# A LoRA feed-forward, grouped-query attention and top-4 mixture of experts in one kernel: the expert rows' table filled in the first stage, three accumulators with deeper rings, activations turned one block later, routing one tile earlier

## The chip, the cores and the metric

The kernel runs on one core of a Trainium2 chip as one program. The metric is the time on the device in microseconds (us); "before" is the median of three runs. The profile is of one execution of its own.

## The reference, cut to what matters

```python
# x: (32, 32, 256): 32 sequences of 32 tokens, T = 1024 tokens of D = 256
def cond(x, Wg, Wu, Wd, A*, B*, idx):        # LoRA with one of 8 adapters per sequence, rank 16, hidden 1024
    gate, up = lora(x, Wg, Ag, Bg, idx), lora(x, Wu, Au, Bu, idx)
    return lora(silu(gate) * up, Wd, Ad, Bd, idx)
def ffn(x, ...):
    h = rms(x, ln_w)
    q, k, v = h @ wq, h @ wk, h @ wv         # 32 heads, 8 kv heads of 64; rope on q and k
    o = softmax(causal(q @ k.T / 8)) @ v
    x = x + o @ wo
    h = rms(x, ff_ln_w)
    logits = h @ wg                          # 16 experts
    topv, topi = top_k(logits, 4)
    weights = scatter(softmax(topv), topi)
    a = silu(h @ w1[e]) * (h @ w3[e])        # for each expert e, 256 -> 256
    return x + sum_e weights[e] * (a @ w2[e])
out = x + ffn(cond(x))
```

## The kernel before, in words

Each engine has an instruction stream written by hand, and semaphores tie them. The order within an engine is the order of the code. Products in float32 are made of a high and a low part (`*_hi`, `*_lo`): three matmuls for one (`product`, L1322).

**Stage A**, to about 122 us: the LoRA feed-forward, on the tokens in two groups of 512. SP loads raw weights into `staging` (`raw`), POOL loads the same weights rounded (`load_hi`) and subtracts (`split`). The last loads of this stage are issued at 69 us; later only four more pieces (`wo_w` 2 and 3, `gate_w`) come through `staging`.

**Stage B**, to about 385 us: eight tiles of 128 tokens (four sequences each). `attend(t)` stands in every engine's stream. On TensorE it makes the scores of tile t, projects q, k and v of tile t + 1, turns the probabilities (`turn_p`), multiplies them with v (`heads_out`), turns the output (`turn_o`, into `oT_hi` by ScalarE and `oT_lo` by VectorE) and makes the output projection (`attention_out`) of tile t - 1. v goes through a DMA that spreads it over blocks by sequence (`spread_v` on SP's queue, into `v_blk`). Softmax works on `z`, which VectorE, POOL (a shift by the maximum) and ScalarE (exponential) touch in turn. For the mixture, older tiles are routed meanwhile: `logits(t - 3)` with `read_logits`, then for t - 4 `hits`, `ranks`, `place` (the position of each token within its expert's rows) and `gates_exp`, `gate_sum`, `pick` (the gate values), then for t - 5 `slots`, `gate_scale`, and on POOL `gates` and four `scatter`, indirect DMAs that write a tile's rows (256 values, 16 gates, the token's number in the row) into `moe_rows` in DRAM. This table has room for 1024 rows for each of 16 experts, and one block for strays, 16512 rows of 276 words. It must hold strays' numbers wherever no token is written, so it is filled beforehand: `fill_rows` on ScalarE's queue, two pieces of 16 x 128 rows in each of `attend(0)` to `attend(3)`, a ninth small one and `set_acc` in `attend(3)`.

**Stage C**, to about 425 us: `send`, `pick` and the others for the last tiles, written out after `attend(6)`; tile 7's attention is written out too.

**Stage D**: 47 blocks of 128 rows. The first 16 are one for each expert in fixed order, the other 31 take their expert and first row from a table that VectorE computes (`blk_exp`, `blk_rows`; `TABLE`, after the gate products of blocks 1 to 3). SP loads a block's rows (`xs<-moe_rows`, a ring of XSR = 6 buffers), TensorE turns them (`rows_in_turned`, L1680), ScalarE and VectorE split them, TensorE multiplies by w1 and w3 (`gate_up_e`, L1326, into `ringT`), ScalarE and VectorE make `mact`, TensorE turns it (`act_turn`, L1699) and multiplies by w2 (`down_e`, L1707). ScalarE scales by the gate (`scaled`, `y`, a ring of YR = 3), and POOL adds it to the accumulator of the block's number mod 2 with an indirect DMA (`moe_acc<-y,xs`, L633; `y_out`). A buffer of xs is free when that DMA has landed, since it holds the token numbers. `value_load` reads an expert's number into TensorE's registers (L1719). The order on TensorE:

```python
for b in range(NBLK + 2):
    if b + 1 < NBLK: rows_in_turned(b + 1)
    if 2 <= b: down_e(b - 2, expert_of(b - 2))
    if 1 <= b <= NBLK: act_turn(b - 1)
    if b < NBLK: gate_up_e(b, expert_of(b))   # expert_of(b): value_load where b >= 16
```

**The end**: SP loads accumulator 1 whole and accumulator 0 in quarters, VectorE adds the one to `resid` and that to the other, SP stores.

Of the kernel before, what the change touches and what calls it, by code (L numbers as in the profile page):

```python
# [14 lines left out]
ALU = mybir.AluOpType  # L15
# [22 lines left out]
MH = HID // P  # L38
NAD = 8
# [25 lines left out]
HXR, XSR, YR = 4, 6, 3  # L65
# [9 lines left out]
def build(nc, x, seq_adapter, cond_head, cond_w, qkv_w, wo_w, gate_w, expert_w, norms, consts, ff_row, route_tab, out):  # L75
    with ExitStack() as ctx:
# [23 lines left out]
        cst = sb("cst", [P, CCOLS])  # L100
        staging = sb("staging", [P, 2, MCOLS])
# [30 lines left out]
        act_hi, act_lo = pair("actp", [P, 2, GROUP])  # L132

# [8 lines left out]
        fill = sb("fill", [P, ROW])  # L142
# [48 lines left out]
        acc_rows = [nc.alloc_sbuf_tensor_at(f"acc_rows{i}", [P, NT, D], F32, offset=qkv_at + 4 * i * NT * D) for i in range(2)]  # L191
        cursor[0] = qkv_at + 4 * NE * WCOLS
        y = sb("y", [P, YR, D])
        mactT = sb("mactT", [P, KD * P])
        assert cursor[0] == probs_end
        ew2 = sb("ew2", [P, NE, W2COLS])
        xs = sb("xs", [P, XSR, ROW])
        xsT_hi, xsT_lo = pair("xsT", [P, 2, KD * P])
        msilu = sb("msilu", [P, D])
        mact = sb("mact", [P, D])  # L200
# [18 lines left out]
        acc_dram = [nc.dram_tensor(f"moe_acc{i}", (T + P, D), F32, kind="Internal").ap() for i in range(2)]  # L219
# [17 lines left out]
        hi_in = [sem(f"hi_in{i}") for i in range(NCH)]  # L237
# [34 lines left out]
        FILLS, ACC_SETS = 9, 3  # L272
# [17 lines left out]
        y_out = [sem(f"y_out{i}") for i in range(2)]  # L290
        acc_in = [sem(f"acc_in{i}") for i in range(1 + NT // 2)]
# [71 lines left out]
        def _(sp):  # L363
# [17 lines left out]

            def spread_v(t):
# [43 lines left out]
            sp.wait_ge(y_out[1], 16 * (NBLK // 2))  # L426
            sp.dma_start(acc_rows[1][:, :, :], acc_tiles[1][:, 0:NT, :]).then_inc(acc_in[0], 16)
            sp.wait_ge(y_out[0], 16 * (NBLK - NBLK // 2))
            for h in range(NT // 2):
                tiles = slice(2 * h, 2 * h + 2)  # L430
                sp.dma_start(acc_rows[0][:, tiles, :], acc_tiles[0][:, tiles, :]).then_inc(acc_in[1 + h], 16)
            for h in range(NT // 2):
                sp.wait_ge(out_rows, h + 1)
                sp.dma_start(out_dram[:, 2 * h:2 * h + 2, :], acc_rows[0][:, 2 * h:2 * h + 2, :]).then_inc(out_done, 16)
# [4 lines left out]
        def _(pool):  # L439
            def load_hi(n):  # L440

                pool.dma_start(chunks[n][1], chunks[n][0]).then_inc(hi_in[n], 16)

            for n in range(4):
                load_hi(n)
                if n == 0:
# [3 lines left out]
                    pool.memset(cst[:, C_EXP:C_EXP + 1], -0.5).then_inc(powers_set, 1)  # L450
                    pool.memset(cst[:, C_EPS:C_EPS + 1], EPS).then_inc(powers_set, 1)
# [4 lines left out]
            def split(n):  # L456
# [3 lines left out]
                pool.wait_ge(hi_in[n], 16)  # L460
# [3 lines left out]
            for n in range(2, FIRST_WO):  # L464
                split(n)
                if n + 2 < FIRST_WO:
# [90 lines left out]
            pool.memset(fill[:, :], 0.0).then_inc(route_ready, 1)  # L557
            pool.memset(all_ones[:, :], 1.0).then_inc(route_ready, 1)
            pool.memset(below_diag[:, :], 1.0).then_inc(route_ready, 1)
            pool.wait_ge(route_ready, 3)  # L560
            pool.iota(fill[:, TOKEN:ROW].bitcast(I32), pattern=[[0, ROW - TOKEN]], base=TRASH, channel_multiplier=1).then_inc(fill_ready, 1)
# [3 lines left out]
            def attend(t, moe=True, rows=True, attn=True, wo=False):  # L565
# [24 lines left out]
            def gates(m):  # L590
# [3 lines left out]
                                   ALU.mult).then_inc(gates_done, 1)  # L594

# [13 lines left out]
            def send(m):  # L609

                gates(m)
                for k in range(TOPK):
# [1183 lines left out]
```

## Time and profile before

| | us |
|---|---|
| median of 3 runs (lowest to highest) | 613.23 (612.27 to 615.87) |
| the profiled execution | 618.39 |
| its span | 616.7 |
| TensorE busy | 496.9 |
| VectorE busy | 333.9 |
| POOL busy | 267.3 |
| ScalarE busy | 192.4 |
| mean granted clock of TensorE | 0.915 |

A granted clock of 1.00 is 2.4 GHz and 0.50 is 1.2 GHz, and a value between is a mixture of the two over the stretch. Times of instructions are read from the profiled execution, which was 5.2 us above the median.

### The profile page before, as it was taken

The numbers are of one execution on the slowest core, as the hardware profiler recorded it, in microseconds if no ns is written. First come the engines' busy times: TensorE is split into PE (matmuls) and PEld (weight loads), VectorE is DVE, ScalarE is ACT, GpSimd is POOL, SyncE is SP. The second block draws the span as 40 slices with busy tenths as digits, with TensorE's granted clock in tenths as the row PEclk, the third lists the DMA queues.
The fourth block names the chain that finished last, engine by engine and source line by source line (L and its number), as shares of the span: only waits on it lengthen the run. The fifth ranks groups of instructions, "written<-read, shape, count | busy, mean of one in ns | idle before, by whom it ended". The sixth has DMA issues, their size and how long they took to land.

```text
span 616.7 us, 8713 instructions
## 1 busy us (share of the span) xinstructions
PE 496.9 (81%) x2819; PEld 415.2 (67%) x2819; DVE 333.9 (54%) x634; ACT 192.4 (31%) x420; POOL 267.3 (43%) x299
## 2 busy tenths in 40 slices
PE   5999999979689992998999958413798888888870
PEld 4888888868579892897988958412576665656540
DVE  3434322466758781888898857132975332333323
ACT  2322232242323330333433233122465332333320
POOL 2877311254553530625454625671354443444440
PEclk9999999997879997899999979855999998999995
DMA  8888400019590929210102192667345444444436
GB/s 294 264 273 256 138 1 2 1 42 328 135 339 22 303 67 349 106 35 2 35 9 63 32 331 76 219 232 276 46 73 88 73 80 70 69 86 72 75 49 214
DMA packets 65229, 80.54 MB, mean 131 GB/s; under 512 B 21009, under 2 KB 55186, under 8 KB 65170
## 3 DMA queue, kind: packets, MB, share of 16 engines
q10 hardware_dynamic: 22608, 33.17, 16.2%
q0 software_dynamic: 11184, 21.06, 15.6%
q1 hardware_dynamic: 31394, 25.76, 15.5%
q8 instruction: 24, 0.39, 0.3%
q14 instruction: 19, 0.16, 0.1%
HBM read 44.51 MB, written 32.32 MB: 125 GB/s over the span
## 4 chain that ended last, share of the span: by engine, by line
PE 48%; DMA 17%; DVE 12%; issue 9%; ACTq 5%; POOL 4%; ACT 3%; SPq 2%; POOLq 0%; DVEq 0%
PE ringA L1326 17%; PE ringT L1326 11%; PE wide L1326 10%; DMA moe_acc<-y,xs 7%; DMA xs<-moe_rows 3%; PE wide L1707 3%; DVE z L1072 2%; PE ringT L1434 2%; POOL moe_rows L536 2%; ACTq L748 2%; DMA v_blk<-v 1%; PE wide L1449 1%; DMA staging<-in_wo_w 1%; DVE oT_lo L1051 1%; DMA head_hi<-in_cond_head 1%
## 5 line engine op out<-in xcount | busy, mean ns | idle before, releaser
L633 POOL DMA_INDIRECT moe_acc<-y,xs x47 | 72.7, 1548 | 109.5 <-ACT y L644 75.8
L498 POOL TENSOR_TENSOR qr<-qc,qs 128x256 f32<-128x256 f32 x80 | 56.7, 734 | 41.9 <-DVE qs L990 41.1
L1326 PE MATMUL ringT<-ew,xsT_hi 128*128 (+1 forms) x188 | 65.3, 429 | 9.5 <-issue 9.3
L1248 DVE TENSOR_TENSOR mact<-msilu,ringT 128x256 f32<-128x256 f32 x47 | 19.7, 419 | 65.7 <-ACT msilu L876 48.4
L1707 PE MATMUL wide<-ew,mactT 128*128 (+1 forms) x188 | 49.4, 386 | 3.3 <-DVE mactT L1243 3.3
L1326 PE MATMUL ringA<-qkvw_hi,hT_hi 128*128 128x512 f32 x96 | 43.6, 454 | 7.2 <-DVE qs L990 6.5
L1326 PEld LDWEIGHTS ringT<-ew,xsT_hi 128*128 128x128 f32 x188 | 33.2, 194 | 20.4 <-issue 15.4
L1326 PE MATMUL ringA<-wo_hi,oT_hi 128*128 128x256 f32 x128 | 40.1, 313 | 1.5 <-issue 1.5
L1680 PE MATMUL wide<-ident,xs 128*128 128x128 f32 x94 | 19.9, 294 | 26.2 <-DMA xs<-moe_rows 26.2
L1326 PE MATMUL ringA<-qkvw_lo,hT_hi 128*128 128x512 f32 x96 | 40.5, 422 | 0.0
L1326 PE MATMUL ringA<-qkvw_hi,hT_lo 128*128 128x512 f32 x96 | 40.5, 421 | 0.0
L536 POOL DMA_INDIRECT moe_rows<-hx,slot x32 | 33.7, 1052 | 14.7 <-issue 9.3
L1326 PE MATMUL ringT<-ew,xsT_lo 128*128 (+1 forms) x94 | 38.0, 404 | 0.0
L1680 PEld LDWEIGHTS wide<-ident,xs 128*128 128x128 f32 x94 | 11.6, 146 | 38.8 <-DMA xs<-moe_rows 20.4
L644 ACT ACTIVATE y<-wide,xs 128x256 f32<-128x256 f32 x47 | 22.3, 474 | 47.4 <-PE wide L1707 39.7
L1707 PEld LDWEIGHTS wide<-ew,mactT 128*128 128x128 f32 x188 | 32.1, 190 | 6.8 <-DVE mactT L1243 3.4
L1326 PE MATMUL ringA<-wo_hi,oT_lo 128*128 128x256 f32 x128 | 36.4, 285 | 0.0
L1326 PE MATMUL ringA<-wo_lo,oT_hi 128*128 128x256 f32 x128 | 36.3, 283 | 0.0
L1449 PE MATMUL wide<-kT_blk,qT_lo 128*128 128x128 f32 x128 | 35.1, 308 | 0.0
L1449 PE MATMUL wide<-kT_blk,qT_hi 128*128 128x128 f32 x128 | 35.0, 308 | 0.0
L1492 PE MATMUL ringT<-ident,o_rows 128*128 128x128 f32 x128 | 20.6, 293 | 17.0 <-DVE oT_lo L1051 16.0
L990 DVE TENSOR_TENSOR qc<-ringA,cst 128x512 f32<-128x512 f32 x40 | 27.4, 685 | 10.0 <-PE ringA L1326 10.0
(236 smaller groups left out, 1349.3 us busy)
## 6 DMA issues: line engine op xcount, KB each, us to landing
moe_rows<-fill ACTq DMA_DIRECT2D x8, 2208.0 KB, 14.3
ew_raw<-in_expert_w ACTq DMA_DIRECT2D x16, 512.0 KB, 6.4
xs<-moe_rows SPq DMA_DIRECT2D x47, 138.0 KB
staging<-in_cond_w SPq DMA_DIRECT2D x8, 576.0 KB, 4.0
cw_hi<-in_cond_w POOLq DMA_DIRECT2D x8, 576.0 KB, 5.5
v_blk<-v SPq DMA_DIRECT2D x32, 128.0 KB
ew<-in_expert_w ACTq DMA_DIRECT2D x16, 256.0 KB, 6.9
qkvw_hi<-in_qkv_w POOLq DMA_DIRECT2D x6, 512.0 KB, 5.7
```

The lines of the kernel that those rows point to most:

```text
L498: last = pool.tensor_tensor(rot[:, :, f, :], cos[:, :, f, :], sin[:, :, 1 - f, :], ALU.add)
L536: pool.indirect_dma_start(out=rows_dram, out_offset=bass.IndirectOffsetOnAxis(slot[:, m, k:k + 1], 0), in_=hx[:, m % HXR, :], in_offset=No ...
L633: pool.indirect_dma_start(out=acc_dram[b % 2], out_offset=bass.IndirectOffsetOnAxis(xs[:, b % XSR, TOKEN:TOKEN + 1].bitcast(I32), 0), in_= ...
L644: return act_e.activation(out, in_, ACT.Copy, scale=scale)
L748: act_e.dma_start(rows_dram[blocks, :].rearrange("(n p) c -> p n c", p=P), fill[:, :].unsqueeze(1).broadcast_to([P, n, ROW])).then_inc(fil ...
L990: last = dve.tensor_tensor(dst[:, c % 2, :].rearrange("p (h d) -> p h d", d=HD), src, table, ALU.mult)
L1248: dve.tensor_tensor(mact[:, :], msilu[:, :], gu_bank[b % 2][:, D:2 * D], ALU.mult).then_inc(m_act, 1)
L1326: mm = pe.matmul(out, a, b, start=first and i == 0, stop=last and i == 2, skip_group_check=True)
L1449: mm = pe.matmul(bank[:, :, s, :], qT[:, a, s, :], k_, start=i == 0, stop=i == 1, skip_group_check=True)
L1492: mm = pe.transpose(ringT[:, a % 2, s * P:(s + 1) * P], o_rows[:, s, a, :], ident[:, :])
L1680: mm = pe.transpose(xs_bank[b % 2][:, k * P:(k + 1) * P], xs[:, b % XSR, k * P:(k + 1) * P], ident[:, :])
L1707: mm = pe.matmul(down_bank[b % 2], mactT[:, k * P:(k + 1) * P], w, start=k == 0, stop=k == KD - 1)
```

## The change

1. The nine fill DMAs and those that set the accumulators move from ScalarE's queue in `attend(0)` to `attend(3)` to SP's queue, behind the last raw load of stage A and ahead of `spread_v(0)`. The tile `fill` is set by POOL at the start. The ring of `hi_in` semaphores becomes five.
2. Three accumulators instead of two, XSR 8 (6), YR 6 (3), `mact` has two buffers.
3. `act_turn` and `down_e` come one block later on TensorE, `act_turned` and `scaled` accordingly; `value_load` of block b + 1 stands behind `gate_up_e(b)`. The experts' weights are split six ahead (three). `expert_in(13)` to `(15)`, that is six DMAs on ScalarE's queue, are issued at block 1 and not ahead of the first rows.
4. Routing: logits for t - 2 (t - 3), hits, ranks, place and pick for t - 3 (t - 4), slots, gate_scale and send for t - 4 (t - 5). Logits and ranks stand at the end of `attend`. The code behind `attend(6)` is written out anew, with one send fewer in it.
5. At the end two accumulators are loaded whole and one in quarters, with two adds over all of `resid`.

```diff
-HXR, XSR, YR = 4, 6, 3
+HXR, XSR, YR, NACC = 4, 8, 6, 3
 # SP, behind the loop of raw loads, ahead of spread_v
+            sp.wait_ge(fill_ready, 2)
+            for i in range(FILLS):
+                rows = slice(16 * i * P, min(16 * (i + 1) * P, SLOTS + P))
+                n = (rows.stop - rows.start) // P
+                sp.dma_start(rows_dram[rows, :].rearrange("(n p) c -> p n c", p=P),
+                             fill[:, :].unsqueeze(1).broadcast_to([P, n, ROW])).then_inc(fill_out, 16)
+            sp.dma_start(acc_dram[0][T:T + P, :], fill[:, 0:D]).then_inc(acc_set, 16)
+            sp.dma_start(acc_dram[0][0:T, :], x.rearrange("b s d -> (b s) d")).then_inc(acc_set, 16)
+            for i in range(1, len(acc_dram)):
+                sp.dma_start(acc_dram[i].rearrange("(n p) d -> p n d", p=P),
+                             fill[:, 0:D].unsqueeze(1).broadcast_to([P, NT + 1, D])).then_inc(acc_set, 16)
 # SP, rows_in
-                    sp.wait_ge(y_out[old % 2], 16 * (old // 2 + 1))
+                    sp.wait_ge(y_out[old % NACC], 16 * (old // NACC + 1))
 # SP, the end
-            sp.wait_ge(y_out[1], 16 * (NBLK // 2))
-            sp.dma_start(acc_rows[1][:, :, :], acc_tiles[1][:, 0:NT, :]).then_inc(acc_in[0], 16)
-            sp.wait_ge(y_out[0], 16 * (NBLK - NBLK // 2))
+            for i, b in enumerate(range(NBLK - NACC, NBLK)):
+                a = b % NACC
+                sp.wait_ge(y_out[a], 16 * (b // NACC + 1))
+                if b < NBLK - 1:
+                    sp.dma_start(acc_rows[a][:, :, :], acc_tiles[a][:, 0:NT, :]).then_inc(acc_in[i], 16)
 # POOL, attend
+                if t >= 3:
+                    pick(t - 3)
                 if t >= 4:
-                    pick(t - 4)
-                if t >= 5:
-                    gates(t - 5)
-                    for k in range(TOPK):
-                        scatter(t - 5, k)
+                    send(t - 4)
 # ScalarE, attend
-                if t == 0:
-                    act_e.wait_ge(fill_ready, 1)
-                if t < 4:
-                    for i in range(2 * t, 2 * t + 2):
-                        fill_rows(i)
-                if t == 3:
-                    fill_rows(FILLS - 1)
-                    set_acc()
 # ScalarE, experts
-            for i in range(3):
+            for i in range(6):
                 expert_hi(i)
-            for i in range(HXR):
-                act_e.wait_ge(hx_out[i], 16 * TOPK * NT // HXR)
-            for i in range(13, NE):
-                expert_in(i)
             rows_hi(0)
-            for b in range(NBLK + 2):
+            for b in range(NBLK + 3):
                 if b + 1 < NBLK:
                     rows_hi(b + 1)
-                if b >= 2:
-                    if b - 2 == NE:
+                if b == 1:
+                    for i in range(13, NE):
+                        expert_in(i)
+                if b >= 3:
+                    if b - 3 == NE:
                         act_e.wait_ge(tab_done, 2)
-                    scaled(b - 2)
-                if b + 3 < NE:
-                    expert_hi(b + 3)
+                    scaled(b - 3)
+                if b + 6 < NE:
+                    expert_hi(b + 6)
 # TensorE, experts
-            for b in range(NBLK + 2):
+            for b in range(NBLK + 3):
                 if b + 1 < NBLK:
                     rows_in_turned(b + 1)
-                if 2 <= b:
-                    down_e(b - 2, expert_of(b - 2))
-                if 1 <= b <= NBLK:
-                    act_turn(b - 1)
+                if 3 <= b:
+                    down_e(b - 3, expert_of(b - 3))
+                if 2 <= b <= NBLK + 1:
+                    act_turn(b - 2)
                 if b < NBLK:
                     gate_up_e(b, expert_of(b))
+                if NE <= b + 1 < NBLK:
+                    expert_of(b + 1)
```

On SP's queue, at the change from stage A to attention, there stood before (raw loads, then `spread_v`):

```order
L367 DMA staging<-in_qkv_w 128x1024 x6
L367 DMA staging<-in_wo_w 128x1024 x2
L388 DMA v_blk<-v 32x16x64 x8
L367 DMA staging<-in_wo_w 128x1024 x2
L367 DMA staging<-in_gate_w 128x32
```

and now:

```order
L370 DMA staging<-in_qkv_w 128x1024 x6
L370 DMA staging<-in_wo_w 128x1024 x2
L389 DMA moe_rows<-fill 128x16x276 x8
L389 DMA moe_rows<-fill 128x276
L391 DMA moe_acc<-fill 128x256
L392 DMA moe_acc<-in_x 16x16384
L394 DMA moe_acc<-fill 128x9x256 x2
L403 DMA v_blk<-v 32x16x64 x8
```

Thirteen DMAs moved in between the raw loads and the first eight of `spread_v`.

On ScalarE, in tile 3 of attention, between two pieces of `oT_hi`, before:

```order
L644 ACTIVATE hT_hi<-ringT,cst 128x128 x2
L643 ACTIVATE oT_hi<-ringT 128x512
L748 DMA moe_rows<-fill 128x16x276 x2
L748 DMA moe_rows<-fill 128x276
L753 DMA moe_acc<-fill 128x9x256
L754 DMA moe_acc<-fill 128x256
L755 DMA moe_acc<-in_x 16x16384
L698 ACTIVATE squares,meansq_62<-resid 128x256
```

and now:

```order
L660 ACTIVATE hT_hi<-ringT,cst 128x128 x2
L659 ACTIVATE oT_hi<-ringT 128x512
L714 ACTIVATE squares,meansq_62<-resid 128x256
L659 ACTIVATE oT_hi<-ringT 128x512 x3
L732 ACTIVATE z<-z 128x512 x2
```

The six DMAs are gone from between the first `oT_hi` and the rest.

On TensorE, in a dynamic block (`ISA` are register instructions that form an address), before:

```order
L1326 MATMUL ringT<-ew,xsT_lo 128x512
L1680 MATMUL wide<-ident,xs 128x128 x2
L1707 ISA
L1707 MATMUL wide<-ew_156,mactT 128x256
L1707 ISA
L1707 MATMUL wide<-ew_156,mactT 128x256
L1699 MATMUL ringA<-ident,mact 128x128 x2
L1719 TENSOR_LOAD blk_exp
```

and now:

```order
L1314 MATMUL ringT<-ew,xsT_lo 128x512
L1704 TENSOR_LOAD blk_exp
L1704 ISA x2
L1665 MATMUL wide<-ident,xs 128x128 x2
L1692 ISA
L1692 MATMUL wide<-ew_158,mactT 128x256
L1692 ISA
L1692 MATMUL wide<-ew_158,mactT 128x256
L1684 MATMUL ringA<-ident,mact 128x128 x2
```

The load of the expert's number moved from behind `act_turn` to behind the last matmul of `gate_up_e`.

## Rows read from the trace of the kernel before

**Rows 1.** The page: busy us (share of the span) xinstructions of each engine.

```profile
PE 496.9 (81%) x2819; PEld 415.2 (67%) x2819; DVE 333.9 (54%) x634; ACT 192.4 (31%) x420; POOL 267.3 (43%) x299
```

**Rows 2.** Windows: us, busy PE, PEld, DVE, ACT, POOL, clock, DMA share, GB/s.

```profile
152.00:188.00 36.00, 28.59 (x138) 24.63 (x137) 24.27 (x40) 9.42 (x17) 20.36 (x21) 0.76 0.77 226
215.50:255.20 39.70, 28.63 (x190) 25.94 (x190) 23.33 (x39) 9.88 (x20) 11.93 (x18) 0.83 0.66 206
255.20:283.80 28.60, 26.87 (x196) 24.55 (x195) 25.18 (x49) 10.39 (x22) 11.95 (x18) 1.00 0.09 19
```

**Rows 3.** Waits of TensorE, 215.5 to 255.2: us in total, times, longest.

```profile
PE ringT L1492 <- DVE oT_lo L1051: 11.1, 1, 11.1
```

**Rows 4.** Timeline of ScalarE's queue: start, duration.

```profile
229.24 9.83 ACTq L748 DMA_DIRECT2D moe_rows<-fill  x3
...
243.58 1.22 ACTq L755 DMA_DIRECT2D moe_acc<-in_x  x1
```

**Rows 5.** Waits of TensorE, 152 to 188.

```profile
PE ringT L1463 <- ACT z L716: 2.7, 2, 2.4
```

**Rows 6.** Timeline of TensorE in the expert stage, from the first to the last block.

```profile
448.91 1.03 PE L1707 MATMUL wide<-ew,mactT 128*128 128x256 f32 x4
449.79 0.44 PE L1699 MATMUL ringA<-ident,mact 128*128 128x128 f32 x2
...
451.69 1.03 PE L1707 MATMUL wide<-ew,mactT 128*128 128x256 f32 x4
...
482.16 0.44 PE L1699 MATMUL ringA<-ident,mact 128*128 128x128 f32 x2
...
596.26 0.44 PE L1699 MATMUL ringA<-ident,mact 128*128 128x128 f32 x2
```

**Rows 7.** Waits of TensorE, 484 to 598.

```profile
PE ringT L1326 <- issue: 8.7, 21, 0.6
PE wide L1680 <- DMA xs<-moe_rows: 8.1, 10, 1.9
```

**Rows 8.** The chain of work, a load in flight; timeline of POOL behind it.

```profile
167.68 7.89 DMA staging<-in_wo_w
...
175.64 2.38 POOL L462 TENSOR_TENSOR wo_lo<-staging,wo_hi 128x1024 fp32r<-128x1024 f32 x1 [0.46 <-DMA staging<-in_wo_w]
```

**Rows 9.** DMA issues of the page: KB each, median us to landing.

```profile
moe_rows<-fill ACTq DMA_DIRECT2D x8, 2208.0 KB, 14.3
staging<-in_wo_w SPq DMA_DIRECT2D x4, 512.0 KB, 4.9
moe_acc<-fill ACTq DMA_DIRECT2D x1, 1152.0 KB, 9.9
```

**Rows 10.** Windows during the fill, columns as in rows 2.

```profile
202.00:216.00 14.00, 12.87 (x87) 11.10 (x86) 11.14 (x18) 4.98 (x10) 7.14 (x11) 1.00 1.07 321
243.00:257.00 14.00, 10.22 (x47) 8.68 (x48) 9.18 (x15) 4.31 (x9) 6.61 (x10) 0.65 0.61 211
```

**Rows 11.** Timelines of SP's queue and of VectorE.

```profile
129.88 37.04 SPq L388 DMA_DIRECT2D v_blk<-v  x8
...
140.63 0.69 DVE L1072 SCALAR_TENSOR_TENSOR z<-wide,cst 128x512 f32<-128x512 f32 x1 [1.88 <-PE wide L1449]
```

**Rows 12.** Timelines of POOL and TensorE at the end of routing.

```profile
391.75 1.07 POOL L536 DMA_INDIRECT moe_rows<-hx,slot  x1 [0.90 <-POOL hx L593]
...
396.68 0.23 POOL L593 TENSOR_TENSOR hx<-picked,ginv 128x16 f32<-128x16 f32 x1
...
425.56 0.66 PE L1680 MATMUL wide<-ident,xs 128*128 128x128 f32 x2 [15.20 <-DMA xs<-moe_rows]
```

**Rows 13.** The chain of work through one turn of the rows ring.

```profile
534.77 0.29 ACTq L886
...
536.65 4.05 DMA moe_acc<-y,xs
...
541.47 2.84 DMA xs<-moe_rows
...
544.36 0.44 PE wide L1680 x2
```

**Rows 14.** Timeline of VectorE at the end.

```profile
608.73 2.29 DVE L1312 TENSOR_TENSOR resid<-resid,acc_rows 128x2048 f32<-128x2048 f32 x1 [11.56 <-DMA acc_rows<-moe_acc]
```

More of the change, by code:

```diff
@@ L132, in build @@
         act_hi, act_lo = pair("actp", [P, 2, GROUP])
+        fill = sb("fill", [P, ROW])
         cursor[0] = overlay
@@ L236, in build @@
         NCH = 1 + MH + QCHUNKS + OCHUNKS + 1
-        hi_in = [sem(f"hi_in{i}") for i in range(NCH)]
+        hi_in = [sem(f"hi_in{i}") for i in range(HI_RING)]
         lo_done = sem("lo_done")
@@ L594, in gates, with send @@
                                    ALU.mult).then_inc(gates_done, 1)
+            def send(m):
+                gates(m)
+                for k in range(TOPK):
+                    scatter(m, k)
             attend(0, moe=False, wo=True)
@@ L608, in _ @@
                 shift(t, half)
-            def send(m):
-                gates(m)
-                for k in range(TOPK):
-                    scatter(m, k)
-            send(t - 5)
-            pick(t - 4)
+            send(t - 4)
             pick(t - 3)
-            send(t - 4)
+            send(t - 3)
             pick(t - 2)
             moe_rows(t - 1)
-            send(t - 3)
             send(t - 2)
@@ L1143, in attend @@
                     outputs_low(t - 1, 3)
-                if t >= 5:
-                    slots(t - 5)
-                    gate_scale(t - 5)
                 if t >= 4:
-                    hits(t - 4)
+                    slots(t - 4)
+                    gate_scale(t - 4)
+                if t >= 3:
+                    hits(t - 3)
                 rope_products(t + 1, 1)
@@ L1294, in _ @@
             TABLE = {1: table_counts, 2: table_owners, 3: table_entries}
-            for i in range(3):
+            for i in range(6):
                 expert_lo(i)
             rows_lo(0)
-            for b in range(NBLK + 1):
+            for b in range(NBLK + 2):
                 if b + 1 < NBLK:
                     rows_lo(b + 1)
-                if b >= 1:
-                    act_turned(b - 1)
-                if b + 3 < NE:
-                    expert_lo(b + 3)
+                if b >= 2:
+                    act_turned(b - 2)
+                if b + 6 < NE:
+                    expert_lo(b + 6)
                 if b < NBLK:
@@ L1309, in _ @@
                     TABLE[b]()
-            dve.wait_ge(acc_in[0], 16)
-            dve.tensor_tensor(resid[:, :, :], resid[:, :, :], acc_rows[1][:, :, :], ALU.add).then_inc(acc_summed, 1)
-            dve.wait_ge(acc_summed, 1)
+            for i, b in enumerate(range(NBLK - NACC, NBLK - 1)):
+                dve.wait_ge(acc_in[i], 16)
+                wait(dve, acc_summed, i)
+                dve.tensor_tensor(resid[:, :, :], resid[:, :, :], acc_rows[b % NACC][:, :, :], ALU.add).then_inc(acc_summed, 1)
+            dve.wait_ge(acc_summed, NACC - 1)
+            last = acc_rows[(NBLK - 1) % NACC]
             for h in range(NT // 2):
                 tiles = slice(2 * h, 2 * h + 2)
-                dve.wait_ge(acc_in[1 + h], 16)
-                dve.tensor_tensor(acc_rows[0][:, tiles, :], acc_rows[0][:, tiles, :], resid[:, tiles, :], ALU.add).then_inc(out_rows, 1)
+                dve.wait_ge(acc_in[NACC - 1 + h], 16)
+                dve.tensor_tensor(last[:, tiles, :], last[:, tiles, :], resid[:, tiles, :], ALU.add).then_inc(out_rows, 1)
         @block.tensor
@@ L1619, in attend @@
                     attention_out(t - 1, QKC + 2)
+                if t >= 2:
+                    bank_read(t - 2, t - 3)
+                    logits(t - 2)
+                if t >= 3:
+                    ranks(t - 3)
             attend(0, before=False, moe=False)
@@ L1637, in _ @@
             attention_out(t - 1, 1, False)
-            bank_read(t - 3, t - 4)
-            logits(t - 3)
-            ranks(t - 4)
             pe.wait_ge(pT_lo_done, 2 * NT)
             rows_turned(t - 2, None)
+            bank_read(t - 2, t - 3)
+            ranks(t - 3)
             heads_out(t)
@@ L1645, in _ @@
             attention_out(t - 1, 3, False)
+            bank_read(t - 2, t - 2)
+            logits(t - 2)
             turn_o(t, 0)
             turn_o(t, 1)
-            bank_read(t - 2, t - 3)
-            logits(t - 2)
-            ranks(t - 3)
             for a in range(2, KVP):
```

132 lines of the change are left out of this document (56 added, 76 removed).

## The prediction

> **What bounds the kernel now.** I read the page first: TensorE is busy for 496.9 of 616.7 us and no other engine for more than 333.9 [rows 1]. So time is won only where TensorE stands idle or runs at the lower of its two clocks, and I looked for these places stage by stage. The windows view takes one tile of attention after another: tile 4 takes 28.6 us at a granted clock of 1.00 and a DMA share of 0.09, tile 3 takes 39.7 us at 0.83 with a share of 0.66, and tile 1 takes 36.0 us at 0.76 with 0.77 [rows 2]. The waits of TensorE then name what came last. In tile 3 it is one wait of 11.1 us for VectorE's oT_lo [rows 3], and the timeline of ScalarE shows what stands behind it: between 229.24 and 244.8 us ScalarE's queue issues three pieces of the table fill and three DMAs that set the accumulators, and does nothing else meanwhile [rows 4]. oT_lo needs ScalarE's oT_hi, whose next piece stands in that queue. In tile 1 TensorE waits 2.7 us in two waits for ScalarE's z [rows 5]. In the expert stage I took the distance between the same instruction of successive blocks: from block 5 to block 15 it is 32.37 us, 3.24 a block, from block 15 to the last 114.10 us for 31 blocks, 3.68 each [rows 6]. Undisturbed, a block takes 2.78 us (448.91 to 451.69, rows 6). The waits of TensorE in the dynamic stretch say "issue" 8.7 us and "DMA xs" 8.1 us [rows 7].
>
> **The fill leaves attention.** Tile 3 without the ScalarE issues should look like tile 4, the nearest undisturbed one: 39.7 - 28.6 = **11.1 us**, which is also the length of the one wait [rows 2, 3]. For tile 1 the fill costs less. POOL splits a wo_w chunk at 175.64 that it waited for [rows 8]; its load took 7.89 us [rows 8] against a median of 4.9 for the four such loads [rows 9], 3.0 us late under the fill's traffic, and the z shift queued behind that split on POOL is what ScalarE's z waits for. I book the 2.7 us of waits [rows 5] and 0.5 for two instructions that then ran at half clock: **3.2 us**. The rest of tile 1's surplus (36.0 - 28.6 - 3.2 = 4.2) I leave: there POOL is busy for 20.36 us against 11.95 [rows 2], with splits of weights that stay where they are.
>
> **The fill on SP.** The same 8 pieces of 2208 KB and their accompaniment (a ninth piece of 138 KB, two accumulators at 1152 KB, a third's 128 KB, 1 MB of x) make 21.3 thousand KB, 21.8 MB. In 202:216, filled with such pieces, the DMA engines moved 321 GB/s [rows 10], so it takes 68 us. SP is free of its loads at 68.8 us: the fill ends about 137. DMA has nothing else in those 60 us, and POOL, ScalarE and VectorE get nothing to issue. Behind it in SP's row is spread_v(0): its first issue stood at 129.88 before [rows 11], its data are wanted by heads_out(0), whose softmax begins at 140.63 on VectorE [rows 11] and takes longer than the 4 us that are left. So **0**, at worst 3. Once SP issues the eight v_blk DMAs, its own queue must have taken the fill's descriptors; the order excerpt of SP shows that the fill stands ahead.
>
> Here a rule of the Trainium skill speaks against the change. The row shows v_blk issued on SP while the fill ran on ScalarE's row, side by side [rows 4, 11]. By the Trainium skill ("DMA: Bandwidth & Descriptors", "Queues, rings and completion order") each issuing engine owns one ring per DMA engine, and descriptors are consumed in ring order, so v_blk now starts only when the fill is through; no run here shows that yet. By the rule the start of attention hangs on the fill's rate alone, and that is rival D below.
>
> **Routing one tile earlier.** Tiles 2 to 6 each still do one logits, one ranks and one set of hits; only the first comes a tile earlier, into tiles 2 and 3 that had none. TensorE's part is 0.8 us of loss, estimated. The gain is in the tail: POOL sends the last five tiles one after the other, four scatters each, at 391.75 and again from 396.68 on, 4.9 us a tile [rows 12], until the first expert rows can be read, and TensorE starts the experts at 425.56 after 15.2 us of idleness [rows 12]. One tile fewer takes 4.9 out of that chain, but gate_scale of the next one comes later than its scatters could start. I take **3.5** (bounds 2 and 6). In exchange expert_in(13 to 15) moves behind the first rows: some 3 us of ScalarE's issue time, beside the table work of VectorE that delays block 1 anyway; I book a loss of **0.5**.
>
> **Static blocks.** With activations turned one block later, act_turn no longer waits for silu and product of the same block. Between blocks 5 and 15 the distance is 3.24, undisturbed 2.78 [rows 6]. I take 2.85: the weight splits (expert_hi, expert_lo) remain on ScalarE and VectorE and keep a little. 10 x 0.39 = **3.9 us**.
>
> **Dynamic blocks.** Here most of it must come, and three things change. (a) The load of the next expert's number stood between act_turn and gate_up (order excerpt), and 21 of 31 blocks show a wait "issue" behind act_turn, 8.7 us together [rows 7]: 0.28 a block. It moves behind gate_up, ahead of the transposed rows of the next block; there some 1.7 us of gate_up's matmuls are queued ahead of it, where before it was the 0.44 of act_turn [rows 6], so most is covered. I keep 0.1. (b) The rows loop. From ScalarE's table read for the y of a block (534.77) through y, the accumulating scatter and the load of xs to TensorE's transpose of those rows (544.36) it is 9.6 us [rows 13]. With 6 buffers the pipeline allows for this three periods less 1.1 us (transposes and down of one turn of the loop, of which down alone is 1.03 in [rows 6]): the period cannot fall below (9.6 + 1.1) / 3 = 3.57, hardly under the 3.68 measured, and the 8.1 us of xs waits are the places where the loop is over [rows 7]. With 8 buffers, of which the later y takes one, four periods less 1.1 are allowed: 10.9 us at a period of 3.0, self limit (9.6 + 1.1) / 4 = 2.67. (c) Scatters into one accumulator follow each other: about 5 us each with a flight of 4.05 [rows 13], over three accumulators 1.7 a block instead of 2.5; no bound either way. YR = 6 does the same for y. Estimate: 2.78 + 0.1 (rest of the value load) + 0.1 (rest of the DMA waits, as the longest single wait was 1.9 us [rows 7]) = 3.0, so 31 x 0.68 = **21.1 us**. From below 2.78 is the floor (27.9 us); from above 3.4, where only (a) and little else works (8.7 us).
>
> At the value load a rule can be weighed against the row. The row says that 21 of the loads left TensorE idle, up to 0.6 us each, in spite of matmuls queued ahead [rows 7]. By the Trainium skill ("TensorE: Matmul & The Clock Gate", "Architectural detail: the array is 16× 32×32, not 1× 128×128", on queue depths) TensorE's queue holds 64 instructions, so that a load with more than 0.5 us of work ahead would be hidden whole. By the row I keep 0.1 a block, by the Trainium skill's depth nothing: 3 us less. The trace agrees in part, 10 loads of 31 show no idleness.
>
> **The end.** Two accumulators of 1 MB come in whole, the third in quarters; VectorE adds the whole one in 2.29 us at 608.73 after waiting for its load [rows 14]. Now two such adds, of which the first waits for an accumulator that was free a block earlier. 1 MB more of loading is 3 us, hidden in part by the earlier start, and the chain of adds is no longer behind the last two scatters but one: I book a gain of **0.5**, between a loss of 2 and a gain of 2.
>
> **The sum**, in the profiled execution: 11.1 + 3.2 - 0.8 + 0 + 3.5 - 0.5 + 3.9 + 21.1 + 0.5 = 42.0. The profiled execution took 618.4 us (its span 616.7 and 1.7 around it), the median of the runs is 613.2, 5.2 lower. 618.4 - 42.0 = 576.4, as a median **571.2 us**. A difference under 0.5% (3 us) could not be told from no change here.
>
> **The rivals.**
> B, the loop does not fall below 3.4 a block: the value load stays exposed at its new place, or each scatter's flight grows as three accumulators let more of them run at once. For it: the flights of 4.05 and 2.84 us [rows 13], which no buffer shortens. Against it: the loop's slack of 1.2 us. Gain 42.0 - 12.4 = 30, **584 us**; chance 0.25.
> C, value load and DMA waits are hidden wholly: period 2.78, 6.8 us more, **564 us**; chance 0.15.
> E, the stall of tile 3 is replaced: with ScalarE free, oT_lo waits for something else, POOL's or VectorE's routing work that came a tile earlier; gain 31, **582 us**; 0.06. For it: VectorE is at 25.2 of 28.6 us in tile 4 [rows 2]. Against: tile 4 has that routing work already and runs at 28.6.
> D, slower: the fill stands in SP's ring ahead of v_blk. Before, its cost was 15 us of stalls [rows 3, 5]; now every us past about 141 delays the whole of attention. With 42 to win it decides from a fill end near 183 us, that is a rate of 190 GB/s instead of 321; 211 GB/s was seen in 243:257, where the queue ran empty in between [rows 10]. At 170 GB/s the fill ends at 197: 56 - 42 = 14 us, **627 us**; 0.04.
> The forecast itself has 0.50.
>
> **The range.** The forecast's own range is 564 to 578 (the bounds of dynamic 2.85 to 3.2, the tail 2 to 6). For 8 in 10 it must take in C and most of B and E: 560 to 588. Faster 0.95 (A, B, C, E less a little), slower 0.04 (D), same 0.01.
>
> **What would show it in the changed profile.** No DMA issue of the fill on ScalarE in attention; tile 3 at about 28.6 us with the clock at 1.00 and no wait over 2 us; tile 1 at about 33. The last fill DMA landed by 137 and no wait for v_blk longer than a us around 141; if TensorE stands there, D's mechanism is at work. The experts start 3 us earlier relative to the last heads_out. Static blocks 2.85 apart, dynamic 3.0, "issue" and "DMA xs" together under 6 us. If the period is above 3.4, the loop is not what I take it for: then the row of TensorE's waits says which of the two was left. The end from the last down to the last output 18 us as before.

## The result and the profile after

The changed kernel takes **569.35 us** (median of 4, 566.74 to 574.67) against 612.75 before in the same comparison: a ratio of 0.9335, 95% interval 0.922 to 0.945. Run again beside the last experiments it took 564.88 us, ratio 0.9255 (0.9216 to 0.9294). The forecast was 571.2 us. The profiled execution has a span of 569.5 us, 47.2 less than before.

From the page of the changed kernel, the same two lines as before [rows 1] and its DMA issue of the fill:

```profile
span 569.5 us, 8712 instructions
PE 483.0 (85%) x2819; PEld 418.3 (73%) x2819; DVE 336.3 (59%) x635; ACT 191.1 (34%) x420; POOL 268.5 (47%) x299
moe_rows<-fill SPq DMA_DIRECT2D x8, 2208.0 KB, 19.8
```

TensorE does the same 2819 matmuls in 14 us less of busy time and stands idle 33 us less. 12 of the 14 us lie in the dynamic blocks (81.45 for 93.30), where the granted clock rose only from 0.98 to 1.00; most of them go because a matmul behind a gap is recorded longer: rings_alone below, at a clock of 1.00 in these blocks, is busy there for 89.92 us. Where the 47.2 us lie, from the starts of heads_out and of the expert rows' transposes in both traces:

| stretch | before | after | difference | forecast |
|---|---|---|---|---|
| start to heads_out(0) | 151.81 | 153.21 | +1.40 | 0 |
| heads_out(0) to (7) | 221.66 | 206.32 | -15.34 | -13.5 |
| of it tile 0 to 1 | 36.20 | 31.74 | -4.46 | -3.2 |
| of it tile 2 to 3 | 39.72 | 28.26 | -11.46 | -11.1 |
| heads_out(7) to first expert rows | 52.09 | 47.70 | -4.39 | -3.5 |
| blocks 0 to 16 | 52.75 | 49.27 | -3.48 | -3.4 |
| blocks 16 to 46 (30 periods) | 109.99 | 83.63 | -26.36 | -20.4 |
| block 46 to the end | 28.40 | 29.37 | +0.97 | -0.5 |

The windows of the changed kernel (columns as in [rows 2]): tile 1, tile 3, tile 4 and the dynamic blocks; below them the dynamic blocks of the kernel before.

```profile
153.20:185.00 31.80, 23.20 (x140) 19.27 (x140) 23.95 (x40) 9.42 (x17) 20.38 (x20) 0.92 0.37 109
211.80:240.10 28.30, 26.95 (x195) 24.56 (x195) 25.11 (x49) 10.39 (x22) 11.98 (x19) 1.00 0.09 20
240.10:268.70 28.60, 26.97 (x198) 24.62 (x197) 24.88 (x51) 10.58 (x24) 12.12 (x19) 1.00 0.09 20
456.50:540.10 83.60, 81.45 (x421) 66.84 (x420) 35.66 (x90) 34.29 (x90) 46.24 (x30) 1.00 0.60 100
...
478.30:588.30 110.00, 93.30 (x420) 67.07 (x421) 36.09 (x89) 35.03 (x89) 44.81 (x29) 0.98 0.46 75
```

Tile 3 is now like tile 4, at a clock of 1.00. In the dynamic stretch TensorE is busy for 81.45 of 83.60 us. Two views of it, its waits and a piece of the chain of work:

```profile
PE wide L1665 <- DMA xs<-moe_rows: 2.1, 2, 1.5
...
490.73 0.22 PE wide L1665 x2
490.94 0.86 PE wide L1692 x4
491.81 0.22 PE ringA L1684 x2
492.03 1.39 PE ringT L1314 x6
493.41 0.22 PE wide L1665 x2
```

The waits named "issue" are gone and those for xs are 2.1 us for 8.1 [rows 7]. The chain is TensorE alone: transposes 0.22, down 0.86, act_turn 0.22, gate_up 1.39, together 2.69 us, and the load of the number leaves no gap in it. Most blocks are 2.70 apart; a few late rows bring the mean of the 30 periods to 2.79.

SP's queue between the raw loads and attention, and VectorE's first product with the scores:

```profile
70.31 52.09 SPq L389 DMA_DIRECT2D moe_rows<-fill  x9
122.44 0.45 SPq L391 DMA_DIRECT2D moe_acc<-fill  x1
...
131.38 6.10 SPq L403 DMA_DIRECT2D v_blk<-v  x4
...
141.66 0.69 DVE L1062 SCALAR_TENSOR_TENSOR z<-wide,cst 128x512 f32<-128x512 f32 x1 [1.41 <-PE wide L1437]
...
133.00:137.00 4.00, 2.54 (x15) 1.76 (x13) 3.75 (x7) 0.97 (x2) 2.14 (x4) 1.00 1.09 373
137.00:141.00 4.00, 3.28 (x21) 3.28 (x21) 1.90 (x4) 2.62 (x5) 2.14 (x6) 0.72 0.68 125
141.00:145.00 4.00, 4.00 (x20) 4.00 (x21) 2.07 (x3) 0.04 (x1) 1.05 (x1) 0.50 0.00 0
```

The DMA engines are full until 137 us and empty from 141 on; VectorE's first z was released by TensorE, not by v_blk. So in this execution the fill was hidden, by about a us. That margin is not safe. In the profiled executions of five experiments below (act_early, load_between, table_late, xsr6 and xsr7), all with the same fill, the same z waited for v_blk, for 1.05 to 2.58 us; xsr7's row:

```profile
140.75 0.69 DVE L1062 SCALAR_TENSOR_TENSOR z<-wide,cst 128x512 f32<-128x512 f32 x1 [2.56 <-DMA v_blk<-v]
```

In the three with two accumulators (fill_only, nacc2 and best) it never waited for v_blk, and heads_out(0) came at 147.3 to 147.5 us, earlier than in any with three (148.2 to 153.2). The third accumulator's 1152 KB stand in SP's queue ahead of v_blk.

### The profile page after: what moved, and what is told of

It reads as the page before. It is cut to its first block, busy times and chain, and to the rows that moved or that the text cites. A ratio compares the mean times of both kernels' runs of the same rounds, so it can differ in the third digit from the quotient of the medians.

```text
span 569.5 us, 8712 instructions
## 1 busy us (share of the span) xinstructions
PE 483.0 (85%) x2819; PEld 418.3 (73%) x2819; DVE 336.3 (59%) x635; ACT 191.1 (34%) x420; POOL 268.5 (47%) x299
## 4 chain that ended last, share of the span: by engine, by line
PE 53%; DVE 14%; issue 11%; DMA 9%; POOL 5%; SPq 3%; ACT 2%; ACTq 2%; another core or an unknown queue 1%; POOLq 0%; DVEq 0%
PE ringA L1314 17%; PE ringT L1314 13%; PE wide L1314 11%; PE wide L1692 4%; DVE z L1062 3%; PE wide L1437 2%; PE ringT L1422 2%; POOL moe_rows L558 2%; DMA moe_acc<-y,xs 2%; DMA xs<-moe_rows 2%; DVE oT_lo L1041 1%; DMA v_blk<-v 1%; SPq L403 1%; DMA acc_rows<-moe_acc 1%; DMA head_hi<-in_cond_head 1%
## 5 line engine op out<-in xcount | busy, mean ns | idle before, releaser
L1314 PE MATMUL ringA<-qkvw_hi,hT_hi 128*128 128x512 f32 x96 | 41.9, 436 | 7.9 <-DVE qs L980 7.2
L1314 PE MATMUL ringA<-qkvw_hi,hT_lo 128*128 128x512 f32 x96 | 39.1, 408 | 0.0
L1314 PE MATMUL ringA<-qkvw_lo,hT_hi 128*128 128x512 f32 x96 | 39.0, 406 | 0.0
L1665 PE MATMUL wide<-ident,xs 128*128 128x128 f32 x94 | 18.7, 285 | 16.4 <-DMA xs<-moe_rows 16.4
L1665 PEld LDWEIGHTS wide<-ident,xs 128*128 128x128 f32 x94 | 13.3, 146 | 23.8 <-issue 14.7
L659 ACT ACTIVATE oT_hi<-ringT 128x512 fp32r<-128x512 f32 x32 | 18.3, 596 | 36.1 <-PE ringT L1480 36.1
```

The costliest lines, as they stand in the source:

```text
L659: return act_e.activation(out, in_, ACT.Copy)
L1314: mm = pe.matmul(out, a, b, start=first and i == 0, stop=last and i == 2, skip_group_check=True)
L1665: mm = pe.transpose(xs_bank[b % 2][:, k * P:(k + 1) * P], xs[:, b % XSR, k * P:(k + 1) * P], ident[:, :])
```

## The experiments

Stretches below are read as in the table above, from one profiled execution of each kernel. The median of the changed kernel was 569.35 and 564.88 us in its two comparisons, so a difference of a few us between medians of different comparisons tells nothing; the ratios stand against the kernel before in the same comparison.

**fill_only**: the kernel before with part 1 of the change alone.

```diff
+            for i in range(FILLS):       # on SP, ahead of spread_v(0)
+                sp.dma_start(rows_dram[rows, :]..., fill...).then_inc(fill_out, 16)
-                    for i in range(2 * t, 2 * t + 2):   # on ScalarE, in attend(t)
-                        fill_rows(i)
```

> The kernel before with one part of the change alone: the fill and the accumulators' setting on SP's queue behind the raw loads of the first stage. My theory (the parts add up, and the fill costs only what stood on ScalarE's queue): the stretch from the first heads_out to the eighth gets 14 to 16 us shorter, as in the changed kernel, the start of attention 0 to 1.5 us later, the expert stage as before at 3.6 to 3.7 us a dynamic block; in all 12 to 15 us less than before, some 599 us. Rival (the gain of attention needs the routing's new places too): less than 8 us.

Measured: 598.61 us, ratio 0.9741 (0.9646 to 0.9835). Heads_out(0) to (7) took 205.81 us for 221.66, so the whole gain of attention comes with the fill; the tail (53.17), the static blocks (52.33) and the dynamic ones (3.68 a block) stayed as before. What the new places of the routing cost attention can't be told: with them it took 203.5 to 212.9 us over twelve profiled executions (206.32 in the changed kernel). The tail is 47.0 to 47.8 us in the kernels that have them and no expert_in(13 to 15) ahead of the first rows, and 49.1 in experts_before_rows below, against 52.1 and 53.2 without the routing's new places: 3 to 4 us are the routing's, and 1.3 to 2.1 the six DMAs'.

**xsr6** and **xsr7**: the changed kernel with fewer row buffers.

```diff
-HXR, XSR, YR, NACC = 4, 8, 6, 3
+HXR, XSR, YR, NACC = 4, 6, 6, 3      # xsr6; xsr7: 4, 7, 6, 3
```

> The changed kernel with the ring of row buffers at 6 and not 8 (y at 6 and three accumulators stay). With y one block later a ring of 6 leaves two periods less 1.1 us for the loop of rows. My theory (the loop of 9.6 us bounds the period by (9.6 + 1.1) / (periods allowed)): 5.3 us a block from block 6 on, 41 blocks x 2.6 = some 105 us more than the changed kernel, 660 to 680 us, slower than before. Rival (the loop is shorter than the 9.6 us or overlaps otherwise, the ring is of no weight): within 10 us of the changed kernel.

> The changed kernel with 7 row buffers: three periods less 1.1 us, the kernel before's allowance. My theory: a period of (9.6 + 1.1) / 3 = 3.57 us in the dynamic blocks, 31 x 0.87 = 27 us more than the changed kernel and 5 to 9 more in the static blocks, 600 to 607 us; nearly the whole gain of the expert stage goes, so that the value load's new place alone is worth little. Rival (the value load was the main price, the ring only the rest): 3.0 us a block, some 580 us.

Measured: xsr6 665.73 us, ratio 1.0822 (1.0708 to 1.0936); xsr7 601.13, ratio 0.9776 (0.9683 to 0.9869). The waits of TensorE in their dynamic blocks, xsr7 first, xsr6 second:

```profile
PE wide L1665 <- DMA xs<-moe_rows: 18.5, 11, 2.9
```

```profile
PE wide L1665 <- DMA xs<-moe_rows: 54.5, 21, 4.9
```

The period was 3.68 us with 7 buffers and 5.45 with 6, against (9.6 + 1.1) / 3 = 3.57 and / 2 = 5.35: the loop of rows sets the period, and each buffer is one period more for it. (The profiled execution of xsr6 was the longest of its four, 674.66 us.) The times fell into the ranges stated, but xsr6 lost 96 us and not 105: its static blocks were 4.35 apart from block 6 on, and not 5.3. xsr7 also shows that with the ring of before, neither the load's new place nor the late turn helps: 3.68 a block, as before.

**nacc2**: the changed kernel with two accumulators and three y buffers.

```diff
-HXR, XSR, YR, NACC = 4, 8, 6, 3
+HXR, XSR, YR, NACC = 4, 8, 3, 2
```

> The changed kernel with two accumulators and a ring of three for y (8 row buffers stay). My theory (a chain of scatters into one accumulator, about 5 us each, gives 2.5 us a block over two and so stays under the 2.70 of the changed kernel): the dynamic blocks stay within 0.1 us of 2.70, and the end gets about 1 to 2 us shorter, since 1 MB less is loaded; 566 to 573 us. Rival (two chains with their queueing are slower than 2.70 a block, 2.9 or more): 575 us or more.

Measured: 567.74 us, ratio 0.9263 (0.9164 to 0.9362). A dynamic block took 2.79 us on the mean, as in the changed kernel (2.79), and block 46 to the end 29.0 us for 29.4, not the 1 to 2 us less that were expected. The third accumulator and the deeper ring of y gain nothing here, and the accumulator's setting may cost 1 to 3 us at the start of attention (the section above; not tested by itself).

**act_early**, **load_between**, **rings_alone**: the changed kernel with the late turn undone, with the load's new place undone, and with both undone.

```diff
 # act_early: TensorE, and accordingly ScalarE and VectorE
-                if 3 <= b:
-                    down_e(b - 3, expert_of(b - 3))
-                if 2 <= b <= NBLK + 1:
-                    act_turn(b - 2)
+                if 2 <= b:
+                    down_e(b - 2, expert_of(b - 2))
+                if 1 <= b <= NBLK:
+                    act_turn(b - 1)
 # load_between
-                if NE <= b + 1 < NBLK:
-                    expert_of(b + 1)
```

> The changed kernel with act_turn and down (and act_turned and scaled) at the kernel before's blocks; 8 row buffers, three accumulators, the load's place and all else stay. My theory (the late turn takes the wait for silu and product out of TensorE's way, which before was small at undisturbed blocks): 2.78 us in the dynamic blocks for 2.70, so 2 to 3 us, and 0.3 us more in each of ten static blocks, where ScalarE's and VectorE's weight splits stand before silu; 573 to 578 us. Rival (the late turn was what let the loop run ahead): above 3.2 us a block, 585 us or more. Second rival (it is worth nothing): within 2 us of the changed kernel.

> The changed kernel with the load of the expert's number between act_turn and gate_up again. Theory of the prediction (its place decides whether it is covered): 0.3 us a block exposed, 9 us more, 577 to 580 us. Rival, which I now hold for likelier (before, TensorE's sequencer stood in act_turn waiting for the product of the same block, and so came late to the load; with the turn one block later it is never held there): no wait named issue in the dynamic blocks, a period of 2.70 to 2.75, 568 to 571 us.

> The changed kernel with the expert stage in the kernel before's order on TensorE (act_turn, down and the number's load at their old places), but with 8 row buffers, 6 for y and three accumulators; the fill, the routing and the rest are changed. Theory (the ring alone makes the gain of the dynamic blocks; with the turn early and the load behind it TensorE's sequencer comes late to the load, and the waits named issue return): 2.78 + 0.3 = 3.0 to 3.1 us a dynamic block, the waits named issue 8 to 9 us, some 577 to 580 us. Rival (these waits too came from the ring's lateness, the load is covered anyway): 2.78 us a block, as with act_early, 568 to 572 us.

Measured: act_early 570.18 us, ratio 0.9289 (0.9238 to 0.9341); load_between 564.99, 0.9224 (0.9149 to 0.9299); rings_alone 590.56, 0.9651 (0.9602 to 0.9700), some 26 us more than the changed kernel beside it. Either of the two edits alone can be left out at no price that the medians show, both together cannot. For act_early the second rival stated came true, as far as the medians tell (570.18 for 569.35), and not my 573 to 578 us: its dynamic blocks have the same mean (2.79), and only its static blocks were longer (51.45 us for 49.27). For load_between the rival that I held for likelier was right on the period and on the wait (2.74 on the mean, no wait named issue); the time lay 3 us below its range. The chain of work in a dynamic block of act_early, of load_between and of rings_alone, and the waits of the last:

```profile
490.21 1.42 PE ringT L1314 x6
491.62 0.22 PE wide L1665 x2
491.84 0.86 PE wide L1692 x4
492.71 0.28 PE ringA L1684 x2
492.99 1.41 PE ringT L1314 x6
```

```profile
490.52 1.40 PE ringT L1314 x6
491.92 0.22 PE wide L1665 x2
492.14 0.87 PE wide L1692 x4
493.01 0.22 PE ringA L1684 x2
493.23 1.39 PE ringT L1314 x6
```

```profile
499.39 1.65 PE ringT L1314 x6
501.04 0.22 PE wide L1665 x2
501.26 0.86 PE wide L1692 x4
502.13 0.28 PE ringA L1684 x2
502.41 0.42 issue
...
PE ringT L1314 <- issue: 13.1, 29, 0.7
```

And what the weight loads of act_turn waited for in rings_alone (first) and in act_early (second):

```profile
PEld ringA L1684 <- DVE mact L1233: 7.4, 30, 0.2
PEld ringA L1684 <- DVE mact L1233: 7.1, 29, 0.2
```

In rings_alone nothing waits for xs; each block has a gap of 0.42 us behind act_turn, and gate_up behind the gap takes 1.65 us for 1.40, so a block costs 3.44 us (2.78 in act_early, 2.70 in load_between). That is the load behind a turn that waits. With the early turn, act_turn waits for VectorE's product in nearly every block, 0.2 us each at most; in the changed kernel and in load_between there is no such wait. In rings_alone the load stands behind this turn in program order, and the gap follows; in act_early the turn waits as long, but the load stands ahead of it, and there is no gap; in load_between the load stands behind a turn that need not wait, and again there is none. Both theories of the run were off in size: 3.0 to 3.1 was too little, 2.78 wrong. The kernel before had two limits lying almost on each other, 3.57 from the ring (worked out; 3.68 in xsr7) and 3.44 from the load.

**experts_before_rows**: the changed kernel with expert_in(13 to 15) ahead of rows_hi(0).

```diff
+            for i in range(HXR):
+                act_e.wait_ge(hx_out[i], 16 * TOPK * NT // HXR)
+            for i in range(13, NE):
+                expert_in(i)
             rows_hi(0)
...
-                if b == 1:
-                    for i in range(13, NE):
-                        expert_in(i)
```

> The changed kernel with the six DMAs of expert_in(13 to 15) on ScalarE's queue ahead of rows_hi(0) again. My theory (at block 1 they stand for 2.7 us on the chain between the rows of block 2 and the weights of expert 6, ahead of the rows they stand partly beside the wait for the first rows): the first block starts its split up to 1 us later, the first six blocks take 2 to 3 us less, in all 1 to 3 us less than the changed kernel. Rival (ahead of the first rows they cost their full 3 us, and at block 1 nothing): 1 to 3 us more.

Measured: 566.43 us, ratio 0.9200 (0.9141 to 0.9260). Blocks 0 to 16 took 46.52 us for 49.27, the stretch ahead of them 49.10 for 47.70. The first load of rows, by the chain of work of this kernel and of the changed one, in this order:

```profile
403.59 4.84 DMA xs<-moe_rows
```

```profile
404.88 2.21 DMA xs<-moe_rows
```

ScalarE issues the experts' weights from 403.20 us on, behind the last scatters, so they share the DMA engines with the first rows, which then take 4.84 us. Both prices show in the profiles, about as expected: 2.75 us gained in the blocks, 1.40 lost ahead of them. The difference of 1.4 us is below what the medians can tell.

**table_late**: VectorE's table behind blocks 9 to 11, and the six DMAs on SP.

```diff
-            TABLE = {1: table_counts, 2: table_owners, 3: table_entries}
+            TABLE = {9: table_counts, 10: table_owners, 11: table_entries}
 # SP, behind rows_in(4), for ScalarE's expert_in at b == 1
+                    sp.wait_ge(m_full, 1)
+                    for i in range(13, NE):
+                        sp.dma_start(ew_raw[e][:, :], ...); sp.dma_start(ew2[:, e, :], ...)
```

> The changed kernel with VectorE's table work behind blocks 9 to 11, where no weights are left to split, and not behind blocks 1 to 3; and expert_in(13 to 15) on SP's queue, behind the fifth load of rows. My theory (VectorE's table and the six DMA issues of ScalarE make the 7 us of stalls in the first six blocks): the 16 static blocks take 44 to 46 us for 49.3, in all 3 to 5 us less than the changed kernel, 564 to 567 us. Rival (the first blocks wait for weights and splits anyway, or the table comes too late for the first dynamic rows): within 2 us of it.

Measured: 567.01 us, ratio 0.9230 (0.9185 to 0.9275). The static blocks took 46.7 us, 2.6 less; the table cost some 3 us at its new place too (three periods of 3.6 to 3.8 us for 2.70), since it holds VectorE's xsT_lo back there as well. About half to two thirds of the expected size showed, and not firmly: best below has the same two edits, and its static blocks took 48.6 us.

**fill_twice**: the fill doubled.

```diff
                 sp.dma_start(rows_dram[rows, :]..., fill...).then_inc(fill_out, 16)
+                sp.dma_start(twice_dram[rows, :]..., fill...).then_inc(twice_out, 16)
```

> The changed kernel with each of the nine fill DMAs doubled, the second one into a table of its own that nobody reads: 18.2 MB more on SP's queue ahead of spread_v(0). Theory of rival D in the prediction (v_blk comes when the fill is through): the fill ends at 190 us for 137, heads_out(0) starts at 190 to 197 us for 153, attention is 38 to 44 us late as a whole, 607 to 615 us, about as slow as before. Rival (v_blk is taken from the queue beside the fill and only shares the engines, as in the kernel before, where it landed in 4.6 us beside a fill): heads_out(0) less than 8 us later, below 580 us.

Measured: 621.73 us, ratio 1.0171 (1.012 to 1.0222), so 1.7% slower than before and above the 607 to 615 expected. SP's queue, VectorE's timeline and a window of this kernel:

```profile
177.25 5.95 SPq L398 DMA_DIRECT2D moe_acc<-fill  x1
183.31 7.88 SPq L407 DMA_DIRECT2D v_blk<-v  x4
...
194.39 0.69 DVE L1066 SCALAR_TENSOR_TENSOR z<-wide,cst 128x512 f32<-128x512 f32 x1 [55.69 <-DMA v_blk<-v]
...
150.00:183.00 33.00, 0.00 (x0) 0.00 (x0) 0.00 (x0) 0.00 (x0) 0.00 (x0) 0.55 1.14 347
```

VectorE waited 55.69 us for v_blk, whose DMAs SP could issue only at 183.31, behind the fill, and for 33 us no engine did anything. Heads_out(0) came at 205.63 us, later than the 190 to 197 expected, since z itself waits for v_blk, and scores, softmax and half-clock matmuls follow the wait. In the kernel before, with a piece of the fill in ScalarE's queue, v_blk of tile 2 landed so:

```profile
200.66 4.56 DMA v_blk<-v
```

**best** and **after_again**: table_late with two accumulators and the load behind act_turn, and the changed kernel beside it.

> table_late with two accumulators (YR stays 6) and the load of the expert's number at its old place behind act_turn, since these two cost nothing in nacc2 and load_between. Expected: 44 to 47 us for the static blocks, 2.70 to 2.75 a dynamic block, the end 0.5 to 1 us shorter; 3 to 5 us less than the changed kernel run beside it. Rival (the three do not add up, since the first dynamic rows now wait for the table): no difference that can be told.

> The changed kernel itself, on the same chip as the three above, to compare with. Expected 565 to 571 us; its start of attention between 147 and 153 us, since the runs so far differ there by the clock of the stretch ahead of it.

Measured: best 565.52 us, ratio 0.9245 (0.9193 to 0.9297); after_again 564.88, 0.9255 (0.9216 to 0.9294). No difference that can be told, where 3 to 5 us less were expected. The dynamic blocks of best run at 2.70 us as expected; its first 16 took 48.6 us, not 44 to 47. In after_again heads_out(0) came at 151.25 us, within the 147 to 153 stated.

## Why the prediction was right, and where its sizes were off

- **The fill leaves attention.** Right: tile 3 by its one wait (11.46 for 11.1). fill_only shows that the fill alone does it. Tile 1 gave 4.46 for 3.2; what I had left out, the half clock behind its stalls, partly went with them (0.92 for 0.76). Over the twelve kernels with a single fill on SP tile 1 took 31.1 to 33.5 us, so its gain is 2.7 to 5.1. Rival E (another wait in place of the old one in tile 3) did not come: tile 3 took 28.26.
- **The fill on SP.** Right in result, wrong in one reading: I took v_blk to be wanted by heads_out(0). VectorE's first z waits for it (fill_twice), so there was no softmax to hide behind, and the margin was the distance from v_blk's landing, before 141, to 141.66. In five experiments it was used up, by 1.05 to 2.58 us; that is within the "at worst 3", for another reason than the one given. Rival D's mechanism is real, and the margin before it small: in fill_twice v_blk was issued 52 us later and the median was 57 us above the changed kernel's. The Trainium skill ("DMA: Bandwidth & Descriptors", "Queues, rings and completion order") says that each issuing queue has its own ring on every DMA engine and that a ring is consumed in order. The rows agree: v_blk came only behind the fill in SP's row, while in tile 2 of the kernel before it landed in 4.56 us beside a fill in ScalarE's. In fill_twice, though, already the issue was held: SP got to v_blk only at 183.31.
- **Routing.** -4.39 for -3.5 in the tail, of which 3 to 4 us are the routing's; the 0.8 booked as a loss in the tiles can't be seen.
- **Static blocks.** -3.48 for -3.4, but by other parts. From block 7 on the period is 2.70 and not 2.85; the first seven take longer than before (25.0 us for 23.1), by expert_in(13 to 15) at block 1, which I booked at 0.5 and which costs about 2.7 there (experts_before_rows), and in part by the table. Two errors that cancel: that the number came out is luck.
- **Dynamic blocks.** The step that was mis-sized: 21.1 us for 31 blocks, which is 20.4 for 30, and measured 26.4 for 30. The loop of rows was right, by formula and number (xsr6, xsr7). The estimate then kept 0.1 for the load and 0.1 for DMA waits above a floor of 2.78; the load is hidden whole, xs waits come to 0.07 a block, and the late turn lowers the floor to 2.70 (act_early keeps 2.78). And part (a) was misread: the 8.7 us of "issue" waits [rows 7] are not what the load costs. They show it in 21 of 31 blocks only, and leave out that gate_up takes 0.25 us longer behind the gap. Without the ring's limit it costs 0.66 a block (rings_alone against act_early), 20 us. Had only the rings been deepened, the period would have been 3.44, which is rival B's 3.4. The load's place is one way to hide it, the late turn another, and with either the mean period came to rival C's 2.78 (2.79).
- **The end.** +0.97 for -0.5, within its bounds; with two accumulators it is 29.0 for 29.4, so the third gains nothing here.
- **The start of attention.** Booked at 0, +1.40 here; in the twelve kernels whose fill is single it lies between 147.3 and 153.2 us (151.81 before). v_blk's wait and the granted clock (last section) both go with the spread; no run tells them apart.
- The sum was 42.0 and the span fell by 47.2; of the difference 6 us are the dynamic blocks. That the median came within 2 us of the 571.2 forecast is partly luck: the profiled execution before lay 5.6 us above its median in this comparison (618.39 for 612.75), the one after only 1.9 (571.28 for 569.35).

## What to carry to other kernels

A ring bounds a loop by (the latency of one turn) / (the periods that the ring leaves to it): work both out from the chain of work before deepening it. Here that told the period to about 0.1 us. Where two limits lie close together, a wait that the profile names beside a larger one is no price of it; undo the edits in pairs, since two that each look worthless may cover for one another. A transfer moved into an idle queue is free only until the next transfer that this queue must carry; look up that one's first reader in the code, and don't guess it from the name.

## What the runs showed of the hardware

- The granted clock in the stretch ahead of attention (122 to 148 us) was 0.80 to 0.82 in some profiled executions (before, after, experts_before_rows) and 1.00 in others (fill_only, nacc2, act_early), and heads_out(0) came at 151.6 to 153.2 in the former and 147.3 to 148.7 in the latter. It is not the clock alone: table_late and xsr7 had 0.95 and 0.94 and came at 151.0 and 152.5, with waits of 2.04 and 2.56 us for v_blk. In the changed kernel the granted clock is 0.72 and then 0.50 from 137 to 145 us, behind the gaps at 133 to 137 in which TensorE is busy for 2.54 of 4.00 us. What decides is open. The spread, some 4 us and up to 6, is larger than what most of the experiments were to show.
- In five of the fourteen profiled executions ScalarE stood for 3.0 to 3.6 us ahead of h2T_hi, eight times in all: in nacc2, xsr6 and xsr7 in the tile from heads_out(5) on and again in the tile behind it, in fill_only and in the changed kernel (at 341.42) once in that later tile. In the other nine never. The timeline of nacc2:

```profile
301.36 0.60 ACT L659 ACTIVATE qT_hi<-ringT 128x512 fp32r<-128x512 f32 x1 [0.56 <-PE ringT L1422]
305.25 0.38 ACT L659 ACTIVATE h2T_hi<-ringT 128x256 fp32r<-128x256 f32 x1 [3.30 <-remote]
```

The trace names no instruction of this core as its releaser. TensorE waited 1.9 us, then ran at a clock of 0.62 from 305 to 318 us, and the tile took 34.3 us for 29.3. A packet of a queue named "instruction" lies within, or in the 0.7 us before, five of the eight waits, but at none of the other three (the changed kernel's and the second ones of xsr6 and xsr7), so a late fetch of instructions does not explain them all; the cause is open.
